# A four-layer graph network on one core: four groups of VectorE operations get a PSUM operand

## Time and profile before

| | |
|---|---|
| median of three runs | 3910.72 us |
| the profiled execution, whole | 3923.71 us |
| its span, first to last instruction | 3921.9 us |
| PE busy | 1905.3 us, 49% of the span |
| DVE busy | 2668.6 us, 68% |
| ACT busy | 2089.4 us, 53% |
| POOL busy | 2730.9 us, 70% |
| mean granted TensorE clock | 0.645 of full speed |
| from the first gather of `entry` to the first of `layer0` | 175.0 to 715.4 us |
| gathers of `layer1` "a", first and last start | 1242.8 and 1747.9 us |
| gathers of `layer1` "b" | 1777.5 and 2298.4 us |
| GpSimd's DMAs in `layer3` | 2895.7 to 3913.2 us |

### The profile page before, as it was taken

How to read it: one execution, slowest core, us unless ns; L and a number is a source line. 1 busy time by engine, 2 the same in 40 slices (tenths; PEclk the granted TensorE clock), 3 DMA queues, 4 the chain that set the end, 5 groups by cost and what they waited for, 6 DMA issues and landing times. The chain is left out here.

```text
span 3921.9 us, 43352 instructions
## 1 busy us (share of the span) xinstructions
PE 1905.3 (49%) x9259; PEld 1501.2 (38%) x9259; DVE 2668.6 (68%) x10026; ACT 2089.4 (53%) x4591; POOL 2730.9 (70%) x2767
## 2 busy tenths in 40 slices
PE   5366610478776878885666646788840000000000
PEld 2133300367775767773444426777830000000000
DVE  8899974477775666655888877899944454444444
ACT  8588820266664222223444545777755555555555
POOL 0177777777774777766777747777737777777776
PEclk9799965688887676665555555766655555555555
DMA  0011177356654666654666645555522222222222
GB/s 7 22 38 38 38 221 226 93 153 162 163 158 138 200 203 202 202 192 142 192 192 202 203 146 174 189 200 191 193 79 80 80 79 74 79 80 80 76 76 59
DMA packets 355520, 521.54 MB, mean 133 GB/s; under 512 B 213243, under 2 KB 224803, under 8 KB 355257
## 3 DMA queue, kind: packets, MB, share of 16 engines
q1 hardware_dynamic: 260936, 363.30, 27.4%
q0 software_dynamic: 94320, 155.47, 17.0%
HBM read 227.56 MB, written 291.01 MB: 132 GB/s over the span
## 5 line engine op out<-in xcount | busy, mean ns | idle before, releaser
L602 POOL DMA_INDIRECT O<-x_pad,nidx x393 | 414.0, 1053 | 119.8 <-issue 119.8
L1155 POOL DMA_INDIRECT l1b_G<-t,src x392 | 402.5, 1027 | 128.9 <-issue 117.5
L1989 PE MATMUL l_psR<-l_diag,l_ones 128*128 128x128 f32 x2 | 0.8, 502 | 1006.6 <-DVE l_diag L1847 1006.6
L1757 POOL DMA_INDIRECT l_G<-t,src x392 | 378.8, 966 | 151.8 <-issue 119.1
L1155 POOL DMA_INDIRECT l1a_G<-t,src x392 | 386.9, 987 | 135.5 <-issue 115.8
L1772 POOL DMA_INDIRECT out<-O,nidx x393 | 390.9, 995 | 128.3 <-issue 118.5
L1464 POOL DMA_INDIRECT l_G<-t,src x392 | 379.4, 968 | 131.5 <-issue 118.7
L850 POOL DMA_INDIRECT l_G<-xs,src x392 | 370.7, 946 | 126.1 <-issue 113.4
L1989 PEld LDWEIGHTS l_psR<-l_diag,l_ones 128*128 128x128 f32 x2 | 0.5, 311 | 1006.7 <-DVE l_diag L1847 1006.7
L174 ACT ACTIVATE O<-O,l_shift,l_rstd 128x96 f32<-128x96 f32 x786 | 292.6, 460 | 27.1 <-DVE l_shift L168 27.1
L1344 PE MATMUL l1a_psP<-l1a_w,l1a_xT 97*128 97x192 f32 x786 | 225.8, 466 | 55.3 <-ACT l1a_xT L1261 55.3
(11 more groups left out here) (334 smaller groups left out, 6407.4 us busy)
## 6 DMA issues: line engine op xcount, KB each, us to landing
h<-l_G SPq DMA_DIRECT2D x96, 392.0 KB, 2.5
t<-l1b_t_out SPq DMA_DIRECT2D x48, 768.0 KB, 3.6
h<-l_G SPq DMA_DIRECT2D x48, 768.0 KB, 3.5
xs<-en_y SPq DMA_DIRECT2D x49, 392.0 KB, 5.2
en_y<-x_pad SPq DMA_DIRECT2D x49, 384.0 KB, 5.0
t<-l_t_out SPq DMA_DIRECT2D x48, 392.0 KB, 4.4
l_H<-t SPq DMA_DIRECT2D x48, 392.0 KB, 3.2
t<-l_tr_out SPq DMA_DIRECT2D x48, 384.0 KB, 3.0
```

What stands on the lines that cost most here:

```text
L602: pool.indirect_dma_start(k.O[:, at, :], None, x, bass.IndirectOffsetOnAxis(k.nidx[:, at:at + 1], 0))\
L1155: pool.indirect_dma_start(tile(c)[:, q, :], None, table, bass.IndirectOffsetOnAxis(k.src[:, at:at + 1], 0))\
L1757: pool.indirect_dma_start(tile(c)[:, q, :], None, t4, bass.IndirectOffsetOnAxis(k.src[:, at:at + 1], 0))\
```

## The change

In `entry` the comparisons read a copy of `iota_hi` in PSUM, the product reads the `iota_lo` that is there already, and the scale factor (`factor`) and the bias row (`b0p`) are put into a new PSUM tile psC. In `layer1` "a" the leaky step leaves `join` and goes behind the transpose: ScalarE's copy of psT to xT now multiplies by 0.01, and a new VectorE operation `leak(t-1)`, placed between `chain(t)` and `join(t)`, takes the maximum of xT (SBUF) and psT (PSUM). `multiply` and the next `turn_rows` wait for `leaked` in place of `copied`, and in TensorE's loop `edges(t+1)` now stands ahead of `multiply(t-1)`. In `layer1` "b" `m` moves to PSUM. In `layer3` the tanh is written to a PSUM tile `tanhs`, which `measure` reads; ScalarE waits for the previous `measure` (`summed`) before it writes it again. No DMA is added, removed or moved in the code.

```diff
@@ entry
+        iota_lo, iota_hi = psI[:, 0:K // 2].bitcast(F16), psI[:, K // 2:K // 2 + 64].bitcast(F16)
+        factor, b0p = psC[:, 0:K], psC[:, K:K + D]
...
-                alike = lambda keys: (k.iota_hi[:, :].unsqueeze(1).to_broadcast([128, n, 128]),
+                alike = lambda keys: (iota_hi.unsqueeze(1).to_broadcast([128, n, 128]),
...
-                column = k.iota_lo if c < NHOT else k.pid
+                column = iota_lo if c < NHOT else k.pid
...
-                                      inv_out[:, c * Q:(c + 1) * Q].unsqueeze(2).to_broadcast([128, Q, D]),
+                                      factor[:, c * Q:(c + 1) * Q].unsqueeze(2).to_broadcast([128, Q, D]),
...
-                                  b0r[:, :].unsqueeze(1).to_broadcast([128, tiles(c), D]), ALU.add)
+                                  b0p.unsqueeze(1).to_broadcast([128, tiles(c), D]), ALU.add)
@@ layer1
-            m = sb("m", [128, Q, D])
+            m = ps("psM", 2)[:, :].rearrange("p (q d) -> p q d", q=Q)[:, :, 0:D]
...
-                dve.drain()
                 if first:
-                    dve.scalar_tensor_tensor(r, r, LEAK, r, ALU.mult, ALU.max).then_inc(joined, 1)
+                    last.then_inc(joined, 1)
...
+            def leak(c):
+                lanes = slice(0, width(c) * 128)
+                dve.wait_ge(copied, c + 1)
+                dve.tensor_tensor(xT[0:D, lanes], xT[0:D, lanes], psT[0:D, lanes], ALU.max).then_inc(leaked, 1)
...
                     chain(t)
+                if first and t >= 1:
+                    leak(t - 1)
...
-                act.activation(xT[0:D, 0:width(c) * 128], psT[0:D, 0:width(c) * 128], ACT.Copy).then_inc(copied, 1)
+                act.activation(xT[0:D, lanes], psT[0:D, lanes], ACT.Copy, scale=LEAK).then_inc(copied, 1)
...
             def turn_rows(c):
-                    pe.wait_ge(copied, c)
+                    pe.wait_ge(leaked, c)
             def multiply(c):
-                pe.wait_ge(copied, c + 1)
+                pe.wait_ge(leaked, c + 1)
...
             for t in range(LAST + 1):
+                if t + 1 < NL:
+                    edges(t + 1)
                 if first and t >= 1:
                     multiply(t - 1)
-                if t + 1 < NL:
-                    edges(t + 1)
@@ layer3
-                dve.tensor_tensor(e_out[:, c % 3, 0:n, :], e_out[:, c % 3, 0:n, :], k.O[:, span(c), :], ALU.add)
+                dve.tensor_tensor(e_out[:, c % 3, 0:n, :], tanhs[:, 0:n, :], k.O[:, span(c), :], ALU.add)\
+                   .then_inc(summed, 1)
...
-                act.activation(e_out[:, c % 3, 0:n, :], e_out[:, c % 3, 0:n, :], ACT.Tanh).then_inc(tanhed, 1)
+                if c >= 1:
+                    act.wait_ge(summed, c)
+                act.activation(tanhs[:, 0:n, :], e_out[:, c % 3, 0:n, :], ACT.Tanh).then_inc(tanhed, 1)
```

More of the change, by code:

```diff
@@ L539, in entry @@
             for i in range(4))
-        psS, psA, psB, psI = ps("psS"), ps("psA"), ps("psB"), ps("psI")
-        iota_lo = psI[:, 0:K // 2].bitcast(F16)
+        psS, psA, psB, psI, psC = ps("psS"), ps("psA"), ps("psB"), ps("psI"), ps("psC")
+        iota_lo, iota_hi = psI[:, 0:K // 2].bitcast(F16), psI[:, K // 2:K // 2 + 64].bitcast(F16)
+        factor, b0p = psC[:, 0:K], psC[:, K:K + D]
         loaded = sem("loaded")
@@ L608, in _ @@
             dve.tensor_copy(psI[:, 0:K // 2], k.iota_lo[:, :].bitcast(F32))
+            dve.tensor_copy(psI[:, K // 2:K // 2 + 64], k.iota_hi[:, :].bitcast(F32))
             dve.tensor_copy(f[:, 0:K], k.src[:, :])
@@ L679, in _ @@
             dve.wait_ge(rooted, 1)
-            dve.reciprocal(inv_out[:, :], inv_out[:, :])
+            dve.reciprocal(factor, inv_out[:, :])
+            dve.tensor_copy(b0p, b0r[:, :])
             dve.wait_ge(tallied, NHOT + 1)
@@ L1090, in layer1 @@
         if first:
-            turned, copied, multiplied = sem("turned"), sem("copied"), sem("multiplied")
+            turned, copied, leaked, multiplied = sem("turned"), sem("copied"), sem("leaked"), sem("multiplied")
             taken_t, taken_r = sem("taken_t"), sem("taken_r")
@@ L1216, in join @@
                     last = dve.tensor_tensor(r, F[:, :, :], r, ALU.add)
-                dve.drain()
                 if first:
-                    dve.scalar_tensor_tensor(r, r, LEAK, r, ALU.mult, ALU.max).then_inc(joined, 1)
+                    last.then_inc(joined, 1)
                 else:
+                    dve.drain()
                     dve.scalar_tensor_tensor(r, r, LEAK, r, ALU.mult, ALU.max)
@@ L1703, in layer3 @@
         psR, psX, psF = ps("psR"), ps("psX"), ps("psF")
+        psY = ctx.enter_context(nc.psum_tensor("l3_psY", [128, 1024], F32))
+        tanhs = psY[:, :].rearrange("p (q d) -> p q d", q=Q)[:, :, 0:D]
         gathered = Landed(k, "l3", SLOTS)
@@ L1725, in layer3 @@
         tanhed = sem("tanhed")
+        summed = sem("summed")
         measured = sem("measured")
```

## The result

Beside the kernel before (3912.6 us, median of 4 runs on the same chip, 3907.7 to 3914.9), the changed kernel took 4055.0 us (median of 4, 4044.5 to 4060.3): ratio of the fast runs 1.0347, 95% interval 1.0327 to 1.0367 (the two medians divide to 1.0364). The profiled execution took 4044.5 us, span 4042.8.

| us | entry | layer0 | layer1 "a" | layer1 "b" | layer2 | layer3 |
|---|---|---|---|---|---|---|
| before | 540.4 | 527.4 | 534.7 | 561.5 | 556.7 | 1017.5 |
| after | 498.4 | 528.5 | 721.7 | 546.0 | 554.0 | 1010.5 |
| difference | -42.0 | +1.1 | +187.0 | -15.5 | -2.7 | -7.0 |

A forecast was written before the change was run, and what follows sets the result against it. POOL's unbroken indirect DMAs were taken to bound every stage, with TensorE's new loop setting layer1 "a"'s pace after the change. -43 + 172 - 12 - 7 = +110 on 3923.7 us, median 13.0 lower: 4021 us, range 3950 to 4085.

The forecast's parts named there:

- Entry, -43 forecast: Entry: gathers no longer held by two-SBUF-operand VectorE operations, 1.053 to 0.944 us over 393; -43 us, bounds -35 and -43.
- Layer1 "a", +172 forecast: Layer1 "a": the swap closes a loop through the edge load, period 14.0 us at the low clock; stage +172 us.
- the landing: Layer1 "a": time for the edge load to land behind two stores, taken as 3.1 us, between 2.1 and 3.8.
- Near 0.5 for the stage: Layer1 "a": sign that the forecast is right, TensorE's granted clock near 0.5 over the stage.
- Layer1 "b", -12 forecast: Layer1 "b": m in PSUM frees held gathers; -12 us, bounds -15 and +5.
- VectorE's cycle of 10.36 us: Layer1 "b": VectorE's own cycle, against POOL's 10.6 us, limits the gain from 15 to 12 us.
- Layer3, -7 forecast: Layer3: 48 scatters no longer held, 1.12 to 0.97 us each; -7 us, bounds -9 and +3.
- The total: Whole kernel: parts sum to +110 us on the profiled 3923.7, median 13.0 lower, 4021 us.
- The bounds of the parts: Low and high per stage: entry -43, -35; layer1 "a" +120, +219; "b" -15, +5; layer3 -9, +3 us.
- The second rival: Layer1 "a": loop stays hidden at 9.0 us, below POOL's 10.0; whole -73, 3838 us; chance 0.13.
- The third: Layer1 "a": loop decides at a mixed clock, period 12.0 us; stage +78, whole +16, 3927 us; chance 0.14.
- The fourth: Whole kernel: one PSUM operand does not release POOL, only layer1 "a"'s loop shows; 4083 us; chance 0.03.

The follow-up runs named there:

- e5: Changed kernel plus 12 filler matmuls per chunk in layer1 "a", between multiply and the wait for edge data: 5301 us, 1.015 to the kernel before.
- f2: Changed kernel with layer1 "a"'s edge load one chunk earlier and POOL waiting for each chunk's gathers to land: 4398 us, 1.122 to the kernel before.
- e4: Changed kernel with TensorE's order in layer1 "a" put back (multiply before edges), moved leaky step kept: 5276 us, 1.010 to the kernel before.
- e1: Kernel before with only TensorE's swap in layer1 "a" (edges ahead of multiply): 5267 us, 1.009 to the kernel before.
- e2: Changed kernel with the edge load of layer1 "a" issued one chunk earlier on SyncE: 5217 us, 1.000 to the kernel before.

## Why the prediction was right

- **Entry, -43 forecast, -42.0 measured.** The mean of 944 came as 947 ns, and POOL stayed last (no idle but its own pause). The last scaling L694 started at 659.6, forecast 660, and the last gather at 665.5, forecast 663.
- **Layer1 "a", +172 forecast, +187.0 measured.** Issue 1.94 us (forecast 2.0), edges 3.63 (3.7), multiply 5.2 in the mean (5.3). The mis-sized term is the landing: 3.5 us in place of 3.1. It was taken between 2.1 and 3.8, and came near the upper end. The sum was 14.1 and was rounded down to 14.0, which is 5 us over the stage. Multiply(0) ended 32.1 us into the stage (forecast 32.6). The 48th take came 666.9 us after the first; with the 4.6 of the short chunks that is 14.29 us a period in place of 14.0, 14 us of the 15 that are missing.
- **The clock.** Right where it mattered, 0.50 to 0.56 during the products. "Near 0.5 for the stage" was the wrong thing to ask: the mean is 0.64 over the stage, since the stretches of waiting count into it at 0.80. TensorE's busy time for the same matmuls says it better: 488.8 us against 421.7.
- **Layer1 "b", -12 forecast, -15.5 measured**, just beyond the bound of -15. Here the reason was not right. The forecast let VectorE's cycle of 10.36 us limit the gain. But POOL never waits for VectorE (its idle time before these gathers is its own pause, 116.0 us, and 16.3 at the start), and (991 + 300) x 8 is 10.33 us, so the gathers still run without a break. The gain is theirs: 392 x (1.027 - 0.991) = 14.1 us, near the 15 that the forecast had before that limit. Some gathers are still held there, as the one beside L1225 (1.43 in place of 0.94): 392 x (0.991 - 0.944) = 18 us in all. Since VectorE's cycle is about as long as the gathers' by now, how much of that could be had is open.
- **Layer3, -7 forecast, -7.0 measured**; the scatter's mean fell from 995 to 979 ns.
- Not forecast: layer0 +1.1, layer2 -2.7, whose code doesn't change.
- **The total.** +110 forecast, +120.9 between the two profiled executions, +142 between the medians. Of the 34 us by which 4021 falls short of 4055, only 11 are in the stages; the other 23 are not the mechanism's. The forecast took the median to lie 13 us below the profiled run, as it did before, and after the change it lies 10.5 above. The bounds of the parts add up to +192 at the top, 4103 us, so the range was cut short at 4085; the result didn't need the difference.
- The second rival (a hidden loop at 9.0 us) needed the shortest landing and the full clock; e5 shows that the full clock alone gives 10.4. The third (mixed clock, period 12.0) did not come: the shortest period with full edge products took 12.8. The fourth fell with entry's 947 ns.

What the prediction left unsaid is that the same order with the load one chunk earlier takes the load off the loop (f2), and that the order of before would not have helped (e4).

## What to carry to other kernels

When two blocks of one engine's loop change places, write down the circle through every queue: here SyncE's in-order queue tied a load to a store, and so to the product that the swap had put behind that load. The load that must land in this loop costs twice, by its 3.5 us and by the clock that TensorE loses (up to 4 us more, by the shortest period of e5). Do the same for the operation that you move: e4's circle goes through VectorE, with no DMA, and is as long. And look for the held indirect DMAs: the gain of 42 us in entry was worked out from two rows.

## What the runs showed beside that

At 5.2 to 5.3 ms the same kernel before was 34 to 36% slower than at 3913 us. Single operations are no longer in e1, which is that kernel but for the swap (full edge products 3.69 us, add 0.95). In e1's entry one round of the one-hot loop took 33.6 us while POOL issued gathers. POOL's last one before a long pause started at 617.50; the waits were still late up to 645.71, and then a round took 3.3 us:

```profile
502.89 0.69 DVE L657 TENSOR_TENSOR O<-iota_hi,en_s_hi 128x512 f16<-128x512 f16 x1 [9.12 <-remote]
...
524.60 0.69 DVE L660 TENSOR_TENSOR O<-iota_hi,en_hi 128x512 f16<-128x512 f16 x1 [21.01 <-issue]
...
536.50 0.69 DVE L657 TENSOR_TENSOR O<-iota_hi,en_s_hi 128x512 f16<-128x512 f16 x1 [9.12 <-remote]
```

```profile
635.91 0.69 DVE L657 TENSOR_TENSOR O<-iota_hi,en_s_hi 128x512 f16<-128x512 f16 x1 [8.43 <-remote]
645.71 0.69 DVE L660 TENSOR_TENSOR O<-iota_hi,en_hi 128x512 f16<-128x512 f16 x1 [9.11 <-remote]
648.40 0.68 DVE L657 TENSOR_TENSOR O<-iota_hi,en_s_hi 128x512 f16<-128x512 f16 x1
651.69 0.68 DVE L657 TENSOR_TENSOR O<-iota_hi,en_s_hi 128x512 f16<-128x512 f16 x1
```

In both places (here and in e2) the late ones wait for counts that TensorE's products raise. Stage "a" of e1 starts the same way. POOL's first 40 gathers run without a break, until 1919.7. The second add starts 29.6 us into the stage (before: 21.9), and the first copy 31 us after the transposes that it waits for ended at 1890.9:

```profile
1899.44 0.95 DVE L1177 TENSOR_TENSOR l1a_G<-l1a_G,l1a_psE 128x768 f32<-128x768 f32 x1 [10.58 <-remote]
...
1921.83 1.02 ACT L1261 ACTIVATE l1a_xT<-l1a_psT 96x1024 f32<-96x1024 f32 x1 [55.09 <-remote]
```

After that, with 5 us without gathers in each period, only one take is late (3.1 us). That unbroken indirect DMAs hold TensorE's signals back on some chips fits this, but was not tested on such a chip; that the lateness outlasts POOL's gathers by 27 us in entry is not explained by it. Why other chips are free of it is open.
